# Per-head score and value products on 64-row tiles, interleaved in two passes, in a fused cross-attention and local-attention transformer kernel

## The reference

```python
def local_attention(q, k, v):
    b, h, n, d = q.shape
    w = WINDOW
    nw = n // w
    ...
    bk2, bv2 = (look(bk), look(bv))      # previous window and own: 64 keys
    ...
    sim = jnp.einsum('bhwie,bhwje->bhwij', bq, bk2) * QK_SCALE
    sim = jnp.where(mask, -jnp.finfo(sim.dtype).max, sim)
    attn = jax.nn.softmax(sim, -1)
    out = jnp.einsum('bhwij,bhwje->bhwie', attn, bv2)
    return out.reshape(b, h, n, d)

def attn_layer(x, Wqkv, qs, ksc, Wo):
    q, k, v = ...                        # x @ Wqkv, 16 heads each
    q = l2norm(q) * qs
    k = l2norm(k) * ksc
    ...                                  # rotary turn and scale of q and k
    return local_attention(q, k, v) @ Wo
```

## Time and profile before

| | us |
|---|---|
| runs (3), median | 1827.32 |
| lowest, highest | 1821.96, 1829.11 |
| the profiled execution | 1824.23 |
| its span in the profile | 1822.2 |
| PE busy | 1750.3 |
| DVE busy | 1619.0 |
| POOL busy | 1500.4 |
| ACT busy | 1327.5 |

### The profile page before, as it was taken

How to read it: one execution, slowest core, us unless ns; L and a number is a source line. 1 busy time by engine, 2 the same in 40 slices (tenths; PEclk the granted TensorE clock), 3 DMA queues, 4 the chain that set the end, 5 groups by cost and what they waited for, 6 DMA issues and landing times.

```text
span 1822.2 us, 48666 instructions
## 1 busy us (share of the span) xinstructions
PE 1750.3 (96%) x18122; PEld 1116.2 (61%) x18122; DVE 1619.0 (89%) x2782; ACT 1327.5 (73%) x2362; POOL 1500.4 (82%) x1204
## 2 busy tenths in 40 slices
PE   7699999999999999999999999999999999999986
PEld 6356666666666666666666666666666666666663
DVE  7799998999999989989999999899999998988874
ACT  3577877877778778778777777787776877877763
POOL 4799888888888888988888888888888888888860
PEclk9999999999999999999999999999999999999998
DMA  4132222222222222322223222222222222222221
GB/s 114 28 87 67 68 71 57 60 73 76 71 63 69 63 66 71 76 65 68 63 56 81 72 70 72 54 63 73 75 72 62 68 58 58 59 71 56 56 64 29
DMA packets 155273, 120.59 MB, mean 66 GB/s; under 512 B 42607, under 2 KB 151457, under 8 KB 154913
## 3 DMA queue, kind: packets, MB, share of 16 engines
q1 hardware_dynamic: 155041, 117.48, 25.1%
HBM read 18.79 MB, written 1.05 MB: 11 GB/s over the span
## 4 chain that ended last, share of the span: by engine, by line
PE 77%; DVE 13%; POOL 5%; issue 3%; SPq 1%; ACT 1%; DMA 1%; DVEq 0%; POOLq 0%; ACTq 0%
PE qk_bank L376 17%; PE ring_bank L448 10%; PE ring_bank L472 9%; PE ring_bank L389 8%; PE sc_bank L423 7%; PE ring_bank L516 6%; PE ring_bank L436 4%; PE ring_bank L399 3%; PE ring_bank L527 3%; PE ring_bank L461 3%; PE ring_bank L410 3%; DVE rn L842 2%; DVE step L837 2%; DVE o L898 2%; DVE qkn L858 2%
## 5 line engine op out<-in xcount | busy, mean ns | idle before, releaser
L1053 POOL TENSOR_TENSOR turned<-qkn,tables 128x512 f32<-128x512 f32 x384 | 489.3, 1274 | 209.8 <-DVE qkn L850 201.5
L1060 POOL TENSOR_TENSOR turned<-qkn,tables 128x512 f32<-128x512 f32 x384 | 496.7, 1294 | 0.0
L376 PE MATMUL qk_bank<-wqkv,xT 128*128 128x512 f32 x768 | 366.5, 600 | 18.8 <-DVE qkn L858 18.6
L1089 POOL TENSOR_TENSOR turned<-turned 128x512 f32<-128x512 f32 x192 | 255.0, 1328 | 15.1
L1096 POOL TENSOR_TENSOR turned<-turned 128x512 f32<-128x512 f32 x192 | 245.1, 1277 | 15.1
L448 PEld LDWEIGHTS ring_bank<-vw,pT 128*32 128x32 f32 x6144 | 156.6, 110 | 143.8 <-issue 143.7
L654 ACT ACTIVATE kB<-ring_bank 64x512 f32<-64x512 f32 x384 | 225.3, 587 | 23.5 <-PE ring_bank L410 21.2
L824 DVE TENSOR_REDUCE ss<-sq 128x16 f32<-128x1024 f32 x192 | 232.0, 1208 | 6.8 <-ACT sq L618 6.8
L627 ACT ACTIVATE vs<-ring_bank 128x512 f32<-128x512 f32 x192 | 114.7, 598 | 163.1 <-PE ring_bank L389 153.4
L898 DVE TENSOR_TENSOR o<-ring_bank,rr 128x512 f32<-128x512 f32 x192 | 132.1, 688 | 104.2 <-PE ring_bank L448 101.3
L389 PE MATMUL ring_bank<-wqkv,xT 128*128 128x512 f32 x384 | 216.1, 645 | 1.6 <-DVE x L978 1.6
(11 more groups left out here) (169 smaller groups left out, 3129.3 us busy)
## 6 DMA issues: line engine op xcount, KB each, us to landing
vw<-vs SPq DMA_DIRECT2D x1152, 64.0 KB, 2.1
vw<-vs SPq DMA_DIRECT2D x672, 32.0 KB, 1.9
wqkv<-in_L_ffn_Wqkv_dram SPq DMA_DIRECT2D x20, 384.0 KB, 3.5
wo<-in_L_ffn_Wo_dram SPq DMA_DIRECT2D x20, 128.0 KB, 3.3
w<-in_L_ffn_W_dram SPq DMA_DIRECT2D x6, 341.0 KB, 3.4
wqkv<-in_L_ffn_Wqkv_dram SPq DMA_DIRECT2D x1, 1536.0 KB, 9.5
x<-in_x_dram SPq DMA_DIRECT2D x2, 512.0 KB, 4.7
out_dram<-x SPq DMA_DIRECT2D x4, 256.0 KB, 2.3
```

Source lines behind the costliest of these rows:

```text
L376: mm = pe.matmul(QK[u % 2][:, i * UW:(i + 1) * UW], tok, wqkv[:, layer % 2, cut:cut + UW], start=True, stop=True)
L1053: return pool.tensor_tensor(heads(turned[:, u % 2, 2 * i, :]), heads(qkn[:, u % 2, i * UW:(i + 1) * UW]), table.unsqueeze(1).to_broadcast( ...
L1060: return pool.tensor_tensor(halves(turned[:, u % 2, 2 * i + 1, :]), halves(qkn[:, u % 2, i * UW:(i + 1) * UW])[:, :, ::-1, :], table.rearr ...
L1089: pool.tensor_tensor(q, q, turned[:, u % 2, 1, :], ALU.add).then_inc(q_summed, 1)
```

## The change

Scores and values are made per head instead of per pair: a product now has 64 rows (one head), 32 columns of weights and 64 moving columns, and its tile position names a row half as well as a strip. There are 32 products per unit and kind instead of 16. `attend` and `scores` are replaced by two passes over both. The first makes the scores of the first head of each pair of unit n-3 (rows 0 to 63) and, in turn with them, the values of the second head of each pair of unit n-5 (rows 64 to 127); the second pass makes the other heads of both. The v projection stands between the passes, and the second pass waits for the first by a new semaphore, `first_half`, which PE raises itself. So the scores stand ahead of the v projection and of the transposes of o, and the value product is complete only behind the v projection.

kB becomes kT and vw loses a dimension, both without zero blocks; ACT copies k with one instruction of 128 rows instead of two of 64. The start-up buffers that lay in vw now lie in kT. The last step of the last layer (`finish`) moves ahead of the value scaling on DVE. The clearing of the buffers changes accordingly.

```diff
@@ (PE)
-            def scores(u):
+            def score(u, k, w, h):
                 g, layer, b, t, half = place(u)
-                pe.wait_ge(mask_done, u + 1)
-                pe.wait_ge(*evicted("q", u))
+                rows, c0 = slice(DH * h, DH * (h + 1)), P * t + WIN * w
+                return pe.matmul(SC_BANK[WIN * w:WIN * (w + 1), (2 * k + h) * DH:(2 * k + h + 1) * DH],
+                                 qT[rows, u % 2, k, WIN * w:WIN * (w + 1)], kT[rows, HP * half + k, c0:c0 + 2 * WIN],
+                                 start=False, stop=True, tile_position=(DH * h, WIN * w), skip_group_check=True)
+
+            def value(u, k, w, h):
+                rows, bank = slice(DH * h, DH * (h + 1)), RING[turns["pv", u] % RINGS]
+                return pe.matmul(bank[WIN * w:WIN * (w + 1), (2 * k + h) * DH:(2 * k + h + 1) * DH],
+                                 pT[rows, u % 2, k, WIN * w:WIN * (w + 1)], vw[rows, u % 2, w, k * DH:(k + 1) * DH],
+                                 start=True, stop=True, tile_position=(DH * h, WIN * w), skip_group_check=True)
+
+            def scores_values(us, uv):
+                s_on, v_on = 0 <= us < UNITS, 0 <= uv < UNITS
+                if s_on:
+                    pe.wait_ge(mask_done, us + 1)
+                    pe.wait_ge(*evicted("q", us))
+                if v_on:
+                    i = turn("pv", uv)
+                    pe.wait_ge(vw_dma[uv % 2], vw_count(uv))
+                    pe.wait_ge(ring_read[i % RINGS], i // RINGS)
+                    pe.wait_ge(*evicted("p", uv))
                 for k in range(HP):
                     for w in range(NW):
...
+                        if s_on:
+                            last_score = score(us, k, w, 0)
+                        if v_on:
+                            last_value = value(uv, k, w, 1)
+                if s_on:
+                    last_score.then_inc(first_half, 1)
+                if v_on:
+                    last_value.then_inc(first_half, 1)
+
+            def scores_values_rest(us, uv):
+                s_on, v_on = 0 <= us < UNITS, 0 <= uv < UNITS
+                pe.wait_ge(first_half, past(min(us + 1, UNITS)) + past(min(uv + 1, UNITS)))
+                for k in range(HP):
+                    for w in range(NW):
+                        if s_on:
+                            last_score = score(us, k, w, 1)
+                        if v_on:
+                            last_value = value(uv, k, w, 0)
+                if s_on:
+                    last_score.then_inc(score_mm, 1)
+                if v_on:
+                    last_value.then_inc(ring_made[turns["pv", uv] % RINGS], 1)
...
                 queries_keys(n)
-                attend(n - 5)
+                scores_values(n - 3, n - 5)
                 values(n)
+                scores_values_rest(n - 3, n - 5)
                 transpose_o(n - 6)
-                scores(n - 3)
                 transpose_p(n - 4)
@@ (ACT)
-            def copy_kB(u):
+            def copy_kT(u):
...
-                for h in range(2):
-                    ev = act.activation(kB[64 * h:64 * h + 64, HP * half:HP * half + HP, h, WIN + P * t:WIN + P * t + P],
-                                        RING[i % RINGS][64 * h:64 * h + 64, :].rearrange("p (k q) -> p k q", q=P), ACT.Copy)
-                ev.then_inc(ring_read[i % RINGS], 1)
+                act.activation(kT[:, HP * half:HP * half + HP, WIN + P * t:WIN + P * t + P],
+                               RING[i % RINGS][:, :].rearrange("p (k q) -> p k q", q=P),
+                               ACT.Copy).then_inc(ring_read[i % RINGS], 1)
@@ (POOL)
-            pool.memset(kB[:, 2:, :, :], 0.0).then_inc(zero_ready, 1)
+            pool.memset(vw[:, :, :, :], 0.0).then_inc(vw_zero, 1)
...
-            pool.wait_ge(b_xT, B)
-            pool.memset(free, 0.0).then_inc(vw_zero, 1)
@@ (SP, v_copies)
-                            sp.dma_start(vw[64 * h:64 * h + 64, k, w, h, :],
+                            sp.dma_start(vw[64 * h:64 * h + 64, k, w, :],
```

More of the change, by code:

```diff
@@ L126, in build @@
         rr = sb("rr", [P, 2, HU])
-        free = vw[:, :, :, :, :].rearrange("p k w h n -> p (k w h n)")
-        def take(start, groups, width):
-            return free[:, start:start + groups * width].rearrange("p (a c) -> p a c", c=width)
-        wx_in, wxT = take(0, 4, C), take(512, 4, C)
-        ctx_sb, vx = take(1024, B, C)[0:CTX], take(1536, B, C)[0:CTX]
-        ctxT, kxT = take(2048, B, CTX), take(2560, B, CTX)
+        chunk = lambda c, groups, width: kT[:, c, WIN:WIN + groups * width].rearrange("p (a c) -> p a c", c=width)
+        wx_in, wxT = chunk(0, 4, C), chunk(1, 4, C)
+        ctx_sb, vx = chunk(2, B, C)[0:CTX], chunk(3, B, C)[0:CTX]
+        ctxT, kxT = chunk(4, B, CTX), chunk(5, B, CTX)
         bcol = sb("bcol", [P, 2])
@@ L234, in build @@
         mask_done = sem("mask_done")
+        first_half = sem("first_half")
         score_mm = sem("score_mm")
@@ L741, in _ @@
                     gelu(g - 2, 2)
-                copy_kB(n - 2)
+                copy_kT(n - 2)
                 if s == 2:
@@ L990, in _ @@
                 if s == 1:
+                    finish(g - 3)
                     centre(g - 2)
```

36 lines of the change are left out of this document (6 added, 30 removed).

## The result

| | before | after |
|---|---|---|
| runs, median us | 1826.37 (4 runs) | 2058.9 (4 runs) |
| lowest, highest | 1821.96, 1829.11 | 2055.14, 2067.6 |
| span in the profile | 1822.2 | 2053.0 |

The changed kernel takes 1.128 of the time, 95% interval 1.124 to 1.133: 232 us more where 152 were forecast (1979 us, range 1930 to 2115). The sign and the mechanism were right; 80 us of size were missing.

What follows compares the result with a forecast made beforehand. The prediction took PE as the bound now and a new loop through DVE, ACT and PE afterwards: +145 us with extras, +7 for Newton steps, +152 on 1824.2, 1976, stated as 1979 us against the runs' median; range 1930 to 2115.

Steps and rivals of the forecast that it cites:

- What bounds the kernel now: PE, busy 96% of the span, was read as the bound, with some half a microsecond a slot to spare over DVE.
- What is bought: Score and value blocks on PE get shorter, 0.43 us each, 0.86 us a slot; passes taken as 0.60 and 0.44 us.
- The loop: From DVE's maxima through qT, first pass, v projection, second pass and value scaling to the next maxima: at least 9.14 us a slot.
- Extras: Added per group of eight slots: 2.25 us in slot 3, 0.84 each in slots 2 and 6, 0.35 for the bias fold.
- the Newton steps: DVE's three small steps, long while POOL works, would become nearly short: +0.3 us a group, +7 us in all.
- edits with no price: ACT's single k copy, POOL's smaller clearings, SP's value copies and the moved last-layer step: taken as nothing.
- My widest feeding bound: Far-end bound for a pass on PE: 64 matmuls at the old mean spacing whatever their length, 1.75 us.
- The passes didn't win: Rival: qT ready when PE asks, so shorter passes gain up to 91 us, 1736 us; chance of faster 0.08.
- Row halves that don't overlap: Rival: PE's row halves don't run side by side, or feeding is slow; passes of 0.87 us, 2111 us; chance 0.13.
- today's spacing: Rival: matmul starts on PE keep their old spacing, passes of 1.75 us, +467 us, 2445 us; chance 0.02.
- POOL stayed out of the way: Rival: POOL stays in the way and DVE's Newton steps keep their present means, 2110 us; chance 0.13.
- The clock's row: Rival: PE's granted clock falls while it idles before the first pass; +125 us in one slot of three, 2103 us; chance 0.04.

Runs made afterwards that it cites:

- experiment 11: The kernel before, with POOL's two sums made on 64 of 512 columns, so part of the work is left out: 1788.67 us, ratio 0.977.
- experiment 1: The changed kernel with ACT copying qT one stage earlier, ahead of the mask fill: 1974.12 us, ratio 1.080 to the kernel before.
- (7): The kernel of experiment 1 with both passes placed ahead of the v projection: 1932.23 us, ratio 1.059 to the kernel before.
- (3): The kernel before with its old 128-row products, put in the order of the change, finish moved too: 2121.55 us, ratio 1.161.
- experiment 2: The kernel before with ACT copying qT one stage earlier, ahead of the mask fill: 1827.41 us, ratio 0.9997.
- 6: The changed kernel with two of four head pairs, leaving out half the scores and value product: 1947.68 us, ratio 1.067 to the kernel before.
- experiment 4: The kernel before in its old order, each score and value product split into two of 64 columns: 1845.56 us, ratio 1.010.
- 9: The kernel of experiment 1 with POOL's two sums on 64 of 512 columns, leaving out work: 1930.87 us, ratio 1.056 to the kernel before.

## Why the prediction was right in sign and 80 us short

**What bounds the kernel now.** Half right. PE has little idle time, but with less work on POOL the kernel before is 39 us faster (experiment 11), so DVE and POOL decided in some slots.

**What is bought.** Overstated. The row halves do run side by side, as taken: eight tiles start within 0.05 us. But the step "I take 0.44 for the second pass, whose instructions can queue behind the v projection" failed. Both passes take 0.64, and the second is as long as the first. The first 32 matmuls start at the pace of the array, whether they waited for qT or for the v projection; the other 32 start two per 0.0165 us. That is 0.24 us a slot, made up for the most part by the 0.20 us that the way from L887 to the first pass came out short.

**The loop.** Right, link by link, in the table and in the timeline, and shown by taking out links: by the medians, qT gives 41 us (1) and the v projection another 79 (7), of which 85 and 42 are left in the time after the holes have changed too; the order alone costs 294 (3), and in the old order a late qT is free (2). Of the signs that I had listed, two came out otherwise: PE's share is 86% and not in the low eighties, and the profile puts the wait before the first pass on "issue".

**Extras, the Newton steps, edits with no price.** Right in the main. Slots 2 and 6 came out 0.28 us longer than summed; the transposes of p wait for L912 179 times, 101.7 us of loads. The Newton steps are short because a slot is longer now. The value copies were in time for the passes, as I said, but not for ACT's v copy, which waits for them for 29.6 us in the changed kernel and 8.8 before. In the 17 slots where it waits over 0.5 us and no hole falls, this costs about 1 us in all; in the kernels that repair the loop it grows. The single k copy and the clearings have no run of their own.

**What I had no term for.** The holes, 56 us, the largest part of what is missing. Nothing in the kernel before shows one inside its blocks; the row of the instruction queue stood on its page, and I did not price 24,576 more instructions against it. My widest feeding bound was about the pace from matmul to matmul, not about the supply behind it. The rest of the sum: 77.7 us a group were forecast, 0.35 of it for the bias fold, which no median holds; the medians sum to 78.3, so passes and PE's string, less what came out shorter, add 0.9, 22 us over 23.9 groups. With 56 us in the slots with holes, 4 in the others, 11 less in the last three slots and 6 more at the two ends of the program that is 152 + 22 + 56 + 4 - 11 + 6 = 229 of the 232.

**The rivals.** The passes didn't win: in plain slots qT is late by more than PE could gain. Row halves that don't overlap, and today's spacing, are refuted by starts 0.007 us apart, eight at a time. The least distance of 25 ns between starts that the Trainium skill states (TensorE: Matmul & The Clock Gate, "Wait — 56ns, not 53.3ns?"), weighed in the prediction, does not hold for matmuls on different tiles here: the trace shows 7 ns. POOL stayed out of the way here, but not in experiments 1, 6 and 7: it is what catches a kernel that repairs the loop. The clock's row kept its nines but for the ends (mean 0.988), although 1.7 us pass between the start of the last q and k matmul and the first pass.

## What to carry to other kernels

When a piece of work moves ahead of others on one engine, write down who makes its input and who waits for its output, and look for a chain that closes on itself; its length is a floor for the period, whatever each engine's busy share says. Here all its pieces stood in the trace of before and summed to 0.1 us of the truth, with two errors of 0.2 us that cancelled.

Matmuls cut into smaller tiles ran at the array's pace here only for the first 64 instructions of a pass. Price the instructions twice, at the pace of feeding and as supply: bursts of 260 instructions within 2.5 us met 48 holes in one order of ACT's work and 17 in another, 128 within 0.95 us none. And when a run changes the time, see by the medians of each slot whether it is the link that you moved: half of what experiment 1 gave back was something else.

Run the suspected cost in the kernel before as well: experiment 2 cleared the old order, and experiment 11 showed that its bound had been read wrongly.

## What the hardware showed that I had not expected

- **A pass has two speeds.** 32 matmuls and 32 loads start at the pace of the array (eight tiles per 0.055 us at 64 columns), the next 32 at two matmuls and two loads per 0.0165 us, about 4 ns an instruction, with 64 columns and with 32. The Trainium skill (TensorE: Matmul & The Clock Gate, "The mechanism") speaks of a reorder window of 64 instructions; the trace agrees in the number, 64 instructions being the point where the pace changes; that the window is the cause no run shows.
- **PE can run dry in the middle of a pass.** 48 holes of 0.5 to 2.0 us, at the edges of blocks of 256 instructions, in a kernel that loads 3.98 MB of them; none with half the products, and none inside the blocks of experiment 4, which loads as much. Each ends 1.24 to 1.57 us behind the end of a packet of the instruction queue.
- **A small operation can wait for a large one on another engine.** DVE's L851, 0.18 us with POOL's sums cut, takes 0.545 us in the mean beside a full POOL (experiments 9 and 1). The Trainium skill (SBUF — State Buffer, "SBUF: two separate sides") states that DVE and GpSimd share a pair of ports under an exclusive lock, taken by a GpSimd operation and, against one that reads SBUF, by a DVE operation with two inputs in SBUF; the runs agree: L851 has both its inputs in SBUF, and the DVE operations of 512 columns that read PSUM keep their 0.68 to 0.69 us.
